# The one-hots of a graph network's adjacency build, laid out by pairs of edge slots

## What is computed

```
def sage_conv(x, src, dst, W_l, b_l, W_r, n_nodes):
    agg = segment_sum(x[src], dst, n_nodes)
    cnt = segment_sum(ones, dst, n_nodes)
    return (agg / maximum(cnt, 1.0)) @ W_l.T + b_l + x @ W_r.T
def _mp_layer(x, src_f, dst_f, ea_f, W, b):
    m = concatenate([x[dst_f], x[src_f], ea_f], axis=1) @ W.T + b
    return relu(segment_sum(m, dst_f, n))
x = layernorm(x + sage(relu(sage(x))))
x = layernorm(x + mp(relu(bn(mp(relu(bn(mp(x))))))))
```

## Time and profile before

| | |
|---|---|
| median of 3 executions | 1293.63 us (1291.86 to 1294.68) |
| profiled execution | 1293.01 us, of which the profile's span is 1291.2 us |
| VectorE busy | 728.6 us (56%) |
| TensorE busy | 1117.8 us (87%) |
| mean granted TensorE clock | 0.891 of full speed |

### The profile page before, as it was taken

One profiled execution on the slowest core, in us unless ns is written; L12 is line 12 of the kernel. 1 busy time (PEld: TensorE's weight loads), 2 busy tenths in 40 slices (PEclk: granted clock), 3 DMA queues, 4 the chain that ended last, 5 costly groups with the idle time before them and its releaser, 6 DMA issues. The chain is left out here.

```text
span 1291.2 us, 20445 instructions
## 1 busy us (share of the span) xinstructions
PE 1117.8 (87%) x8160; PEld 667.1 (52%) x8160; DVE 728.6 (56%) x1452; ACT 341.6 (26%) x626; POOL 89.4 (7%) x102
## 2 busy tenths in 40 slices
PE   0358878998689879999999999999789998899994
PEld 0358878897688534445455554444334444334442
DVE  6799999999998302121244356654455655324344
ACT  2444565566666100000000001011231012300000
POOL 4111211211111000000000000000000000000001
PEclk9966767877557889999999999999889999989997
DMA  6223343556565897575357760765503765107660
GB/s 157 59 65 115 118 152 116 196 177 202 181 226 199 333 344 243 231 265 202 117 195 282 289 233 13 285 243 225 200 13 124 299 244 226 75 21 293 247 239 19
DMA packets 69304, 240.84 MB, mean 187 GB/s; under 512 B 31760, under 2 KB 44811, under 8 KB 53747
## 3 DMA queue, kind: packets, MB, share of 16 engines
q1 hardware_dynamic: 62276, 191.48, 41.6%
q0 software_dynamic: 6928, 48.00, 9.9%
HBM read 197.66 MB, written 41.79 MB: 185 GB/s over the span
## 5 line engine op out<-in xcount | busy, mean ns | idle before, releaser
L1141 PE MATMUL PM<-Aring,Xop 128*128 128x512 fp8e4 (+1 forms) x2450 | 498.1, 363 | 0.0
L1141 PEld LDWEIGHTS PM<-Aring,Xop 128*128 128x128 f16 x2450 | 227.3, 98 | 266.8 <-issue 16.3
L637 PE MATMUL PW<-key,lo 128*128 128x52 fp8e4 (+2 forms) x2466 | 200.2, 258 | 10.2 <-ACT F L698 10.2
L637 PEld LDWEIGHTS PW<-key,lo 128*128 128x128 fp8e4 x2466 | 189.6, 122 | 18.3 <-ACT F L698 11.2
L1141 PE MATMUL PM<-Ares,Xop 128*128 128x512 fp8e4 x735 | 171.5, 389 | 9.3 <-DMA Ares<-adj 7.1
L1596 ACT ACTIVATE F<-PH,bag 64x512 f32<-64x512 f32 (+1 forms) x39 | 25.4, 657 | 382.3 <-PE PH L1324 382.2
L1434 DVE TENSOR_TENSOR S<-PM,rc 128x256 f32<-128x256 f32 (+1 forms) x50 | 18.7, 414 | 190.0 <-PE PM L1141 149.1
L1141 PEld LDWEIGHTS PM<-Ares,Xop 128*128 128x128 f16 x735 | 70.7, 100 | 100.2 <-issue 13.1
L652 PE MATMUL PA<-Ares,ea 128*128 128x32 f16 x1867 | 112.1, 234 | 0.1
L652 PEld LDWEIGHTS PA<-Ares,ea 128*128 128x128 f16 x1867 | 109.1, 118 | 0.2 <-issue 0.2
L1436 DVE TENSOR_SCALAR S<-PM 128x256 f32<-128x256 f32 (+1 forms) x75 | 31.4, 418 | 130.4 <-PE PM L1141 118.5
(11 more groups left out here) (136 smaller groups left out, 950.5 us busy)
## 6 DMA issues: line engine op xcount, KB each, us to landing
Aring<-adj SPq DMA_DIRECT2D x90, 1568.0 KB, 9.8
adj<-Xop POOLq DMA_DIRECT2D x12, 1568.0 KB, 5.8
adj<-stage POOLq DMA_DIRECT2D x12, 1568.0 KB, 6.2
Ares<-adj SPq DMA_DIRECT2D x6, 1568.0 KB, 15.8
rc<-rc_d SPq DMA_DIRECT2D x24, 256.0 KB, 9.9
rc<-ea_sum SPq DMA_DIRECT2D x36, 128.0 KB, 5.7
Aring<-adj SPq DMA_DIRECT2D x5, 784.0 KB, 4.4
eaf<-in_erow SPq DMA_DIRECT2D x62, 51.0 KB
```

The lines of the kernel that those rows point to most:

```text
L637: last = nc.tensor.matmul(PW[bank % RING][:, c:c + 52 * (z - y)].rearrange("p (u b) -> p u b", b=2), lo[:, h % 2, i, :].bitcast(f8), key[: ...
L1141: last = nc.tensor.matmul(o, x[:, h, :], rhs, start=h == 0, stop=h == NT - 1)
```

## The change

`SEGS` now lists one product `key` per destination digit `d` instead of one per width; a slot of width w has its columns in w of these blocks. Digit 0 is two blocks, one for the slots that have more digits and one for the rest. Inside a block the layout is pairs of slots, 26 values, the two slots of the pair. So the columns of one slot stand 2 elements (4 bytes) apart, whatever the block's length. The number of elements in all blocks stays (105,274 before, 105,300 now), and their instructions go from 92 to 120. `H` gets the same layout (64 pairs, 26 values, 2), and its one-hot reads the first two of the 16 equal numbers that the table `io` holds for each value; from one value to the next these stand 32 bytes apart. The table `iop` shrinks from 32x32 to 32x2 numbers. `cnt_early` moves from a buffer of its own into `Ares`, and for that the load of the first stages also waits until the counts have been stored (`s_cd`).

```
-    _left = sorted(range(_h * HS, min(NS, _h * HS + HS)), key=lambda k: -SLOT[k][3])
...
-    for _w in range(4, 0, -1):
-        _n = sum(SLOT[k][3] >= _w for k in _left)
...
-            _segs.append((_i, _n, _w, _at))
...
+    _n = [pairs(sum(SLOT[k][3] > d for k in _k)) for d in range(4)]
+    _step = 26 * _n[1]
+    _segs = [(d, 0, _n[d], d * _step) for d in (1, 2, 3) if _n[d]] + ([(0, 0, _n[1], 0)] if _n[1] else [])
...
+        _segs.append((0, _n[1], _n[0] - _n[1], _at))
...
-        cnt = sb("cnt_early", [16, EARLY // 16])
+        cnt = within(0, [16, EARLY // 16], f32)
-        iop = within(0, [128, PD, CH], i16)
+        iop = within(0, [128, PD, 2], i16)
-        H = within(1, [128, 2, 26, 128], u16)
+        H = within(1, [128, 2, HS, 26, 2], u16)
...
                     sp.wait_ge(s_lo, NCH)
+                    sp.wait_ge(m["s_cd"], 16)
...
-                onehot(H[:, t % 2], 26, 16, d[:, 2])
+                shape = [128, HS, 26, 2]
+                nc.vector.tensor_tensor(
+                    H[:, t % 2], io[:, 16:42, 0:2].rearrange("p v (o e) -> p o v e", o=1).broadcast_to(shape),
+                    d[:, 2].rearrange("p (q o e) -> p q o e", o=1, e=2).broadcast_to(shape), ALU.is_equal)
...
-                for i, n, w, o in SEGS[h][0]:
-                    last = outer(key[:, h % 2, o:o + 26 * w * n], Dv[:, t % 2, 0:w, at + i:at + i + n],
-                                 H[:, t % 2, :, at + i:at + i + n], w, 26, n)
+                for d, i, n, o in SEGS[h]:
+                    o, i = o + h % 2 * QW, i + at
+                    last = nc.vector.tensor_tensor(
+                        key[:, o:o + 26 * n].rearrange("p (q v e) -> p q v e", v=26, e=2),
+                        Dv[:, t % 2, d, i:i + n].rearrange("p (q o e) -> p q o e", o=1, e=2).broadcast_to(
+                            [128, n // 2, 26, 2]), H[:, t % 2, i // 2:(i + n) // 2], ALU.mult)
...
-                nc.vector.tensor_tensor(ohd[:, r, :, 0:n], iop[:, :, 0:n],
...
+                shape = [128, PD, CH // 2, 2]
+                nc.vector.tensor_tensor(
+                    ohd[:, r].rearrange("p d (q e) -> p d q e", e=2),
+                    iop[:].rearrange("p d (o e) -> p d o e", o=1).broadcast_to(shape),
+                    vd[:, c % 2].rearrange("p (o q e) -> p o q e", o=1, e=2).broadcast_to(shape), ALU.is_equal)
```

More of the change, by code:

```diff
@@ L69, with pairs @@
 LAST_OF = [max(k for k in range(NS) if SLOT[k][2] // 8 == b) for b in range(NBK)]
+def pairs(n):
+    return n + n % 2
 ORDER = []
@@ L75 @@
 for _h in range(NH):
-    _left = sorted(range(_h * HS, min(NS, _h * HS + HS)), key=lambda k: -SLOT[k][3])
-    _at, _i, _segs = 0, 0, []
-    for _w in range(4, 0, -1):
-        _n = sum(SLOT[k][3] >= _w for k in _left)
[L80 to L84, removed]
-            _segs.append((_i, _n, _w, _at))
-            _left, _i, _at = _left[_n:], _i + _n, _at + 26 * _w * _n
-    SEGS.append((_segs, _at))
-QW = max(_at for _, _at in SEGS)
+    _k = sorted(range(_h * HS, min(NS, _h * HS + HS)), key=lambda k: -SLOT[k][3])
+    _n = [pairs(sum(SLOT[k][3] > d for k in _k)) for d in range(4)]
+    _step = 26 * _n[1]
+    _segs = [(d, 0, _n[d], d * _step) for d in (1, 2, 3) if _n[d]] + ([(0, 0, _n[1], 0)] if _n[1] else [])
+    _rest = 26 * (_n[0] - _n[1])
+    _hole = [(at + 26 * n, 26 * (_n[1] - n)) for _, _, n, at in _segs if _n[1] - n]
+    _at = next((at for at, size in _hole if size >= _rest), max((at + 26 * n for _, _, n, at in _segs), default=0))
+    if _rest:
+        _segs.append((0, _n[1], _n[0] - _n[1], _at))
+    for _i, _x in enumerate(_k):
+        PLACE[_x] = (_i, _i // 2 * 52 if _i < _n[1] else _at + (_i - _n[1]) // 2 * 52, _i % 2, _step)
+    ORDER += _k
+    SEGS.append(_segs)
+QW = max(at + 26 * n for segs in SEGS for _, _, n, at in segs)
 RW = 448
@@ L255, in build @@
         lo = sb("lo", [128, 2, HS, 64], u16)
-        key = sb("key", [128, 2, QW], u16)
+        key = sb("key", [128, 2 * QW], u16)
         packed = m["F"][:].bitcast(u16).rearrange("p (r c) -> p r c", r=4)
@@ L319, in wide @@
         def wide(t):
-            return max(w for h in (2 * t, 2 * t + 1) if h < NH for _, _, w, _ in SEGS[h][0])
+            return max(d + 1 for h in (2 * t, 2 * t + 1) if h < NH for d, _, _, _ in SEGS[h])
         block = ctx.enter_context(nc.Block(no_gpsimd_drain=True))
@@ L331, in _ @@
             sp.dma_start(io[:], ins["c_io"].rearrange("p (a b) -> p a b", b=16)).then_inc(s_io, 16)
-            sp.dma_start(iop[:], ins["c_iop"].rearrange("p (a b) -> p a b", b=CH)).then_inc(s_io, 16)
+            sp.dma_start(iop[:], ins["c_iop"].rearrange("p (a b) -> p a b", b=2)).then_inc(s_io, 16)
             sp.dma_start(pb[:], ins["c_pb"].broadcast_to([128, NPS])).then_inc(s_io, 16)
@@ L500, in small @@
                 valued(Dv[:, t % 2, 0:w], D[:, 0:w], w, d[:, 5]).then_inc(s_sm, 1)
[L502 to L506, removed]
             def large(h):
@@ L547, in attributes @@
                                             pb[:, c * CH:c * CH + n], ALU.subtract))
-                nc.vector.tensor_tensor(ohd[:, r, :, 0:n], iop[:, :, 0:n],
-                                        vd[:, c % 2, 0:n].rearrange("p (o s) -> p o s", o=1).broadcast_to([128, PD, n]),
-                                        ALU.is_equal)
+                shape = [128, PD, CH // 2, 2]
[3 more added lines that the diff above has]
+                    vd[:, c % 2].rearrange("p (o q e) -> p o q e", o=1, e=2).broadcast_to(shape), ALU.is_equal)
                 v.wait_ge(s_hi, c + 1)
@@ L612, in turn, with columns @@
                 last.then_inc(s_tp, 1)
+            def columns(buffer, o, odd, step, w):
+                if w == 1:
+                    step = 52
+                if buffer:
+                    end = QW + o + (w - 1) * step + 52
+                    x = key[:, end - w * step:end].rearrange("p (d v e) -> p d v e", d=w, e=2)[:, :, step // 2 - 26:]
+                else:
+                    x = key[:, o:o + w * step].rearrange("p (d v e) -> p d v e", d=w, e=2)[:, :, 0:26]
+                return x[:, :, :, odd:odd + 1].bitcast(f8)
             pe.wait_ge(s_id, 16)
@@ L629, in _ @@
                             pe.wait_ge(s_wev, bank - RING + 1)
-                    i, x, o, n = PLACE[k]
+                    i, o, odd, step = PLACE[k]
                     if start:
@@ L635, in _ @@
                     for y, z in cuts:
-                        c, o2 = y % 8 * 52, o + 26 * n * (y - qa)
+                        c = y % 8 * 52
                         last = nc.tensor.matmul(
[L638 to L641, removed]
+                            PW[bank % RING][:, c:c + 52 * (z - y)].rearrange("p (d v b) -> p d v b", d=z - y, b=2),
+                            lo[:, h % 2, i, :].bitcast(f8), columns(h % 2, o + (y - qa) * step, odd, step, z - y),
                             start=start, stop=stop and z == qa + w)
@@ L1709 @@
     arr["c_io"] = np.tile(np.repeat(np.concatenate(steps).astype(np.int16), 16), (128, 1))
-    arr["c_iop"] = np.tile(np.repeat(np.arange(PD, dtype=np.int16), CH), (128, 1))
+    arr["c_iop"] = np.tile(np.repeat(np.arange(PD, dtype=np.int16), 2), (128, 1))
     arr["c_pb"] = np.array([PD * w for w, _ in PSLOT], np.int16)[None, :]
```

## The result

The changed kernel takes 1308.42 us (median of 4 executions, 1306.20 to 1309.47), the kernel before 1293.97 (4 executions). The ratio is 1.0112, with a 95% interval of 1.0094 to 1.0130: slower by 1.1%. Its profiled execution has a span of 1306.9 us, against 1291.2.

The account below looks back on a forecast made before the run. VectorE's list was taken to bound the build to about 402 us, before a 27 us TensorE tail and SyncE's loads. 19.4 + 2.0 - 3 - 2 = +16.4 us on 1293.0 gave 1309 us, range 1300 to 1317.

Parts of the forecast that it names:

- the case of 70%: Whole kernel: the forecast of 1309 us itself, between 1304 and 1315 us, given 70%.
- What bounds the build: Build up to about 402 us: lasts as long as VectorE's list of work, VectorE being busy 97% from 60 us.
- `H`: +19.4 us: VectorE's 16 one-hots `H`: 1664 pairs at 0.73 ns more each for the 32-byte step, +19.4 us (bounds 0 and +23.4).
- The rest of VectorE: +2.0: VectorE's other new forms: 28 more `key` products +2.2, lost surcharge -0.5, last `ohd` +0.3, together +2.0 us.
- Waits of VectorE: -3: VectorE in the build: three waits for `eax`, one before `lo` and those for TensorE go, -3 us (bounds 0, -3.3).
- The tail and the first loads: -2: Build's end: TensorE ends 6 to 8 us sooner, loads go out at the same point, -2 us (bounds +2, -6).
- The layers: 0: `layers` behind the first loads and the wait for `F`: no term of their own in the sum.
- Rival 1: `H` on VectorE: the 32-byte step is free and all else holds, -3 us, 1290 us; 14%.
- Rival 3: VectorE's waits and the tail: surcharge holds, but each gives back 6 us, +9.4 us, 1302 us; 11%.
- rival 2: `H` on VectorE: loses the rate of two elements per step, +27.8 instead of +19.4 us, 1318 us; 5%.
- One sign: TensorE's slots' matmuls: a full run of 104 columns under 80 ns from one to the next; 93 means no layout effect.

Follow-up runs that it names:

- run 3: The kernel before with two more one-hots of 128x1024 in each `small`, nothing else: 1315.66 us, ratio 1.0161.
- run 1: The changed kernel with `H` reading a table of its own whose 26 values stand 4 bytes apart instead of 32: 1287.70 us, ratio 0.9944 to the kernel before.
- run 2: The changed kernel with the 16 one-hots `H` reading in turn from tables of step 4, 8, 12, 16 and 32 bytes; executed once, only for the one-hots' lengths.
- run 6: The kernel before with only `iop` of 32x2, the early counts inside `Ares` and the wait for their store: 1296.63 us, ratio 1.0030.
- run 4: The changed kernel with the early counts in the third part of `Ares`, `B` in the first, and no SyncE wait for the counts' store: 1309.09 us, ratio 1.0112.
- the compact kernel: The changed kernel with a table for `H` whose values stand 4 bytes apart: 1287.70 us (0.9944 to the kernel before), repeated at 1288.14 us (0.9955).

## Why the prediction was right

1309 us were forecast, 1308.4 measured; the case of 70% came true. The deciding term, `H`, was right in mechanism and size. That the total fits to 1 us is partly luck: between the profiled executions VectorE's list came out 1.0 us longer than forecast, the tail gave 3.8 us more, and the layers ended 2.1 us later, which nearly cancels (15.7 us measured, 16.4 forecast). Each step beside its row:

- **What bounds the build.** VectorE's list up to its last half: shown by run 3, which lengthens it alone, and by run 1, in which TensorE was quicker throughout and VectorE's last half did not move.
- **`H`: +19.4 us.** Measured 20.0 (50.2 - 30.2 us). The surcharge read off two products of 208 elements, 0.73 ns a reading, is 0.75; a time made of the number of elements alone would have left `H` at 1885 ns. In the trace the start of `lo` stands behind its counterpart of before by 1.9, 3.2, 4.5, 5.7 us and so on, one step of 1.25 us with each `small`. Runs 1 and 2 show that it is the step in bytes of the table and not the pattern of the one-hot.
- **The rest of VectorE: +2.0.** The products `key` went from 64.3 to 65.6 us busy, and `ohd` took 0.3 behind them: 1.6. Up to the last half VectorE is busy for 20.9 us more.
- **Waits of VectorE: -3.** Mis-sized: `eax` was waited for 8.2 us instead of 8.7, and of the short waits before `lo` 0.9 us went, so -1.4. Two waits at the start, which I had left alone, nearly cancel: the one for `Xop` fell from 6.7 to 5.5 us and the one for the first gather (`in_dst`) grew from 5.9 to 6.6. All idle time of VectorE up to its last `key` fell by 1.5 us. The whole list came out at 20.9 - 1.5 = +19.4, forecast +18.4. Whether the shorter `iop` did anything for it is not shown; run 6 has the short table and is 0.5 us late there.
- **The tail and the first loads: -2.** The direction of each piece was right, their sum mis-sized: the distance falls from 19.4 to 13.6 us, -5.8. TensorE's tail gave 7.7, as forecast (6 to 8), and the new wait cost SyncE 7.9 us, not 4.0, because the store of the counts stood behind two stores of 1.57 MB. So the loads did not go out "at the same point as before" but 4.2 us later against VectorE's list. What I had not seen is that this costs little (run 4): before, TensorE had 3.64 and 3.05 us of waits for `F` and the third block, which took up the late start. Nor did I count TensorE's clock: behind those waits it had been 0.50 into the third block, and that it is 1.00 there now is 1.6 us of the 5.8. In the kernel before, where the stores are not crowded, the same wait costs 2.7 us with the other small edits (run 6).
- **The layers: 0.** 2.1 us come on top after the third block, 1.9 of them between 928 and 1133 us, in stretches that the change does not touch. TensorE's granted clock is the larger part: where a new layer begins (930 us with the change, 918 before) it is 0.5 for 13.7 us instead of 10.2. Single executions of one kernel differ as much: in the two traces of the compact kernel (run 1 and its repeat) it is 10.2 and 13.7 us there, and from the third block to the end their distance to the kernel before changes by 0.0 and by +2.0 us. So these 2.1 us are no sign of the change.

Rival 1 (free at 32 bytes, 1290 us) is what run 1 makes true by another table: 1287.7. Rival 3 was right that the tail gives more than 2 us, but VectorE's waits did not shrink as it has them; rival 2 has nothing for it. One sign was set too simply: a full run of 104 columns was to lie under 80 ns a matmul, but the one shown takes 83, because it ran mostly at half clock (45 and 86 ns at either level).

## What to carry to other kernels

A layout that suits the engine that reads it is paid for by the engine that writes it: look for the new step of every operand, the small constant tables too, and keep at least two readings in each 16 bytes. A quicker TensorE gains nothing while it waits for VectorE; it gains behind VectorE's last instruction, and only that stretch is to be counted, down to the transfers and waits that follow from it. A wait before a large load can be almost free where the DMA engines are full, and the load held back lets small stores land that others wait for; the next barrier decides what a held load costs.

## What the runs showed of the hardware

- All three engines take about the same for a reading far enough from the one before it: VectorE 1.04 + 0.75 = 1.79 ns, TensorE 1.79 to 1.87 ns, ScalarE at most 1.92. That the piece is 16 bytes was measured on VectorE alone (run 2); the steps of the other two were 64 bytes and more. On TensorE it does not depend on the clock: 104 columns in 52 places took 94 ns at full clock and 95 ns at half. Only with the columns 4 bytes apart did its clock matter for these matmuls (45 and 86 ns).
- TensorE, idle for longer in the middle, kept the same mean clock there: 0.70 in both kernels. Where it stood 3.64 us for `F` in `layers`, the granted clock was 0.50 from 460.5 to 470.7 us, and 49 matmuls of 512 columns that began there took 12.32 us instead of 10.75.
- A store of 14 KB took 4.0 us to land behind one store of 1.57 MB and 7.7 us in the changed kernel, behind two. It landed 0.4 and 0.2 us after the last of these (423.27 and 422.90 us before, 443.06 and 442.89 now):

```profile
rc_d<-Ares SPq DMA_DIRECT2D x1, 14.0 KB, 7.7
```
